# Inverse sums behind the third mask, four PSUM banks for the last batch's turns, and bounds of experts read ahead of the routed loop

## The reference, cut to what matters

```python
x = x + self_attention(layernorm(x), w_atten, w_proj)   # 16 heads of 32, rope on q and k, causal softmax
x = x + cross(layernorm(x), ctx)                        # energy = (ctx Wq + bq)(ctx Wk + bk)^T, softmax,
                                                        # then layernorm(x) @ attention: tokens are mixed
h = layernorm(x)
shared = silu(h @ Ws_gate) * (h @ Ws_up) @ Ws_down      # inner width 704, every token
scores = softmax(h @ W_router)                          # 8 experts, the best 2 of each token
routed = sum over the 2: score * ffn_e(h)               # inner width 352
x = x + routed + shared
```

## Time and profile before

| | us |
|---|---|
| median of 3 runs | 995.3 (993.45 to 995.39) |
| the profiled execution | 993.71, its span 991.9 |
| PE busy | 954.6 (96%) |
| DVE busy | 624.6 (63%) |
| ACT busy | 492.1 (50%) |
| POOL busy | 207.1 (21%) |

### The profile page before, as it was taken

One profiled execution on the slowest core, in us unless ns is written; L12 is line 12 of the kernel. 1 busy time (PEld: TensorE's weight loads), 2 busy tenths in 40 slices (PEclk: granted clock), 3 DMA queues, 4 the chain that ended last, 5 costly groups with the idle time before them and its releaser, 6 DMA issues.

```text
span 991.9 us, 18270 instructions
## 1 busy us (share of the span) xinstructions
PE 954.6 (96%) x6147; PEld 770.8 (78%) x6147; DVE 624.6 (63%) x1644; ACT 492.1 (50%) x1289; POOL 207.1 (21%) x247
## 2 busy tenths in 40 slices
PE   8989899999999999999799999999999999999998
PEld 6457666766667676666588888899999999999997
DVE  5699777867878667787665676524443344425565
ACT  1478865746657466567843331334443344432221
POOL 3222212221122211120000002222322222203342
PEclk9999999999999999999999999999999999999999
DMA  9765754338643375446900121745534542515554
GB/s 244 116 99 75 157 111 66 57 50 241 122 65 54 51 208 114 65 65 225 317 27 22 61 78 54 268 151 172 162 103 144 172 152 88 170 50 162 169 174 157
DMA packets 69981, 124.94 MB, mean 126 GB/s; under 512 B 6352, under 2 KB 22992, under 8 KB 69904
## 3 DMA queue, kind: packets, MB, share of 16 engines
q1 hardware_dynamic: 63440, 104.81, 42.5%
q0 software_dynamic: 5600, 18.35, 6.4%
q10 hardware_dynamic: 864, 0.79, 0.5%
HBM read 70.19 MB, written 28.57 MB: 100 GB/s over the span
## 4 chain that ended last, share of the span: by engine, by line
PE 80%; DVE 9%; DMA 4%; issue 3%; ACT 3%; POOL 1%; DVEq 0%; ACTq 0%; POOLq 0%
PE ps L1432 26%; PE ps L1442 14%; PE ps L1181 8%; PE ps L1341 5%; PE ps L1279 5%; PE ps L1233 5%; PE ps L1220 3%; DMA ks<-rope_a 3%; PE ps L1256 3%; PE ps L1206 3%; PE ps L1450 2%; PE ps L1420 2%; PE ps L1122 1%; DVE probs L1617 1%; DMA qs<-rope_b 1%
## 5 line engine op out<-in xcount | busy, mean ns | idle before, releaser
L1617 DVE CUSTOM_DVE_ANT_0 probs<-ps,mask 128x128 f32<-128x128 f32 (+3 forms) x256 | 122.3, 486 | 64.6 <-PE ps L1220 32.9
L910 ACT COPY probsT<-ps 128x128 f32<-128x128 f32 (+3 forms) x256 | 108.7, 425 | 103.5 <-PE ps L1233 64.2
L902 ACT ACTIVATE probs<-probs,nb 128x128 f32<-128x128 f32 (+3 forms) x256 | 146.6, 573 | 23.9 <-DVE nb L1622 23.4
L1220 PE MATMUL ps<-ks,qs 96*128 96x256 f32 (+2 forms) x256 | 127.1, 500 | 10.1 <-DVE mx L1617 7.5
L1233 PE MATMUL ps<-ident,probs 128*128 128x128 f32 x640 | 112.8, 275 | 1.6 <-ACT probsT L910 1.4
L1028 ACT ACTIVATE sg<-ps 128x352 f32<-128x352 f32 x69 | 32.0, 464 | 159.8 <-PE ps L1432 158.3
L1233 PEld LDWEIGHTS ps<-ident,probs 128*128 128x128 f32 x640 | 78.7, 141 | 26.9 <-issue 18.9
L1922 DVE TENSOR_TENSOR hidden<-sg,ps 128x352 f32<-128x352 f32 x69 | 35.8, 519 | 95.7 <-ACT sg L1028 95.7
L781 POOL TENSOR_TENSOR rope_a<-rope_a,sin_sb 128x512 f32<-128x512 f32 (+1 forms) x34 | 41.2, 1210 | 226.4 <-DVE rope_a L1599 226.4
L1220 PEld LDWEIGHTS ps<-ks,qs 96*128 96x128 f32 x256 | 48.5, 190 | 49.9 <-DVE mx L1617 21.2
L1926 DVE TENSOR_TENSOR h_lo<-ps,h_hi 128x384 fp32r<-128x384 f32 x68 | 37.9, 557 | 74.3 <-ACT h_hi L1032 73.6
(11 more groups left out here) (226 smaller groups left out, 2139.8 us busy)
## 6 DMA issues: line engine op xcount, KB each, us to landing
gu_raw<-in_we SPq DMA_DIRECT2D x10, 1408.0 KB, 6.6
y_d<-y_sb SPq DMA_DIRECT2D x37, 256.0 KB, 2.8
shared_x<-xT_d SPq DMA_DIRECT2D x32, 256.0 KB
qs<-rope_b SPq DMA_DIRECT2D x30, 256.0 KB, 5.7
ks<-rope_b SPq DMA_DIRECT2D x30, 256.0 KB, 5.7
d_raw<-in_we SPq DMA_DIRECT2D x10, 512.0 KB, 8.3
attT<-in_wpT SPq DMA_DIRECT2D x4, 1024.0 KB, 8.6
acc<-in_x SPq DMA_DIRECT2D x4, 1024.0 KB, 10.8
```

The source lines that it names most:

```text
L902: nc.scalar.activation(pr, pr, ACT.Exp, bias=nb[:, n % 2, h:h + 1], scale=SCALE, accum_out=sums[:, n % 2, h:h + 1]).then_inc(exp_done, 1)
L910: nc.scalar.copy(probsT[n % 2][:, h, 0:w], ps[:, T_BANK + h % 2, 0:w]).then_inc(pT_done, 1)
L1220: nc.tensor.matmul(ps[:, S_BANK + h % 2, 0:w], stacks[G % 2][0][:, h, i * P:(i + 1) * P], stacks[G % 2][1][:, h, 0:w], start=True, stop=Tr ...
L1617: nc.vector.tensor_tensor_reduce(probs[n % TT][:, h, 0:w], ps[:, S_BANK + h % 2, 0:w], mask[:, TOKENS - w:], 1.0, LOWEST, ALU.add, ALU.max ...
```

## The change

Five edits. First, `invert(n)` on DVE moves from ahead of the second mask (h = 1) to behind the third (h = 2) of the same step. Second, the last batch's turns of attention, second norm and third norm take four banks instead of two (`LAST_BANKS`: X_BANK, X_BANK + 1, T_BANK, O_BANK), so that tile t no longer waits for tile t - 2; the waits move to the reader before in the same bank: turns of the second norm wait for the attention copy of their own tile, turns of the third for the second norm's copy of their own tile, and `mix` waits for each tile's second copy. Third, LAST_CROSS changes places: attention turns, scales and second turns come up to a place sooner, the second energy a place later, the split of the projection's weights one or two places sooner. Fourth, PE, ACT and DVE read the end of expert 0 at FFN place 44, and of later experts one bound instead of two (the old end is the new beginning); SP still reads both. Fifth, on PE the second routed tile of expert 0 is written out ahead of the loop, and its gate, up and turn stand ahead of the wait for the last shared sum.

```diff
 LAST_CROSS = dict(
-    CROSS, context=(2, 7), context_copy=(7, 9), energy=(10, 11, 14, 15), energy_max=(10, 11, 14, 15),
+    CROSS, context=(2, 7), context_copy=(7, 9), energy=(10, 12, 14, 15), energy_max=(10, 12, 14, 15),
     energy_exp=(12, 14, 15, 16), energy_divide=(14, 18, 19, 20),
-    split_projection=(5, 6, 8, 10), split_y=(14, 14, 15, 16),
+    split_projection=(4, 5, 6, 8), split_y=(14, 14, 15, 16),
     project=((16, 16, 17, 18), (18, 18, 19, 19), (20, 20, 21, 21), (22, 22, 23, 23)), add_projected=(18, 20, 22, 24),
-    second_stats=(19, 21, 23, 25), second_variance=(26,), attention_turn=(25, 26, 27, 27), attention_copy=(25, 26, 27, 28),
-    second_scale=(28, 28, 29, 29), second_turn=(30, 30, 31, 31), second_copy=(30, 31, 31, 32),
+    second_stats=(19, 21, 23, 25), second_variance=(26,), attention_turn=(25, 25, 26, 26), attention_copy=(25, 26, 26, 27),
+    second_scale=(27, 28, 28, 29), second_turn=(29, 29, 30, 30), second_copy=(29, 30, 30, 31),
     mix=((33, 33, 34, 34), (35, 35, 36, 36), (37, 37, 38, 38), (39, 39, 40, 40)), add_mixed=(35, 37, 39, 41),
     third_stats=(36, 38, 40, 42), third_variance=(43,), third_scale=(45, 45, 46, 46), third_turn=(47, 47, 48, 48),
...
+        LAST_BANKS = (X_BANK, X_BANK + 1, T_BANK, O_BANK)
+
+        def turn_bank(p, t):
+
+            return LAST_BANKS[t] if p == BATCHES - 1 else X_BANK + t % 2
+
         def second_bank(p, t):
-            return X_BANK + (t % 2 if p == BATCHES - 1 else 1)
+            return LAST_BANKS[t] if p == BATCHES - 1 else X_BANK + 1
         SPLIT_PLACES = tuple((BATCHES - 1) * PLACES + at for at in (51, 52, 53, 55, 65, 67))
...
+        RANGE_PLACE = 44
+
+        def first_end(eng):
+
+            eng.wait_ge(slots_ready, 2)
+            return eng.value_load(first_i[0:1, 1:2], min_val=LEAST, max_val=ROUTED_TILES)
+
+        def next_end(eng, e):
+
+            return eng.value_load(first_i[0:1, e + 1:e + 2], min_val=LEAST, max_val=ROUTED_TILES)
+
         x_v = x.rearrange("(b t p) d -> b p t d", p=P, t=TT)
         out_v = out.rearrange("(t p) d -> p t d", p=P)
...
                         nc.scalar.copy(dst[:, :, t * P:(t + 1) * P],
-                                       ps[:, X_BANK + t % 2, :].rearrange("p (c n) -> p c n", c=TT)).then_inc(done, 1)
+                                       ps[:, turn_bank(p, t), :].rearrange("p (c n) -> p c n", c=TT)).then_inc(done, 1)
                     for t in tiles_at(since, 0, when["second_copy"]):
                         if p:
...
                     for t in tiles_at(since, 0, when["third_copy"]):
-                        copy_turned(norm3, p, t, xn_xT[:, t, :, :], X_BANK + t % 2, norm3.copied)
+                        copy_turned(norm3, p, t, xn_xT[:, t, :, :], turn_bank(p, t), norm3.copied)
                     if since in when["router_copy"]:
                         act.wait_ge(r_mm, p + 1)
...
                     hidden_high(shared, j - 1)
+                if place == RANGE_PLACE:
+                    hi = first_end(act)
                 if place in SILU_PLACES:
                     nc.scalar.activation(silu_unused[:], bias_sb[:, 0:1], ACT.Silu)
...
             hidden_high(shared, TILES - 1)
-            act.wait_ge(slots_ready, 2)
             for e in range(EXPERTS):
-                lo, hi = block_range(act, e)
-                if e == 0:
-                    lo = 0
+                lo, hi = (hi, next_end(act, e)) if e else (0, hi)
                 act.wait_ge(raw_loaded, (e + 3) * RAW)
                 split(e + 2, e % 2, range(SOONER))
...
                         pe.wait_ge(norm2.copied, p * TT + t)
-                elif t < 2:
-                    pe.wait_ge(aT_done, p * TT + t + 3)
                 else:
-                    pe.wait_ge(norm2.copied, p * TT + t - 1)
+                    pe.wait_ge(aT_done, p * TT + t + 1)
                 turn_tile(norm2, p, t, second_bank(p, t))
...
                     pe.wait_ge(xm_added, p * TT + t + 3)
+                elif p < BATCHES - 1:
+                    pe.wait_ge(norm3.copied, p * TT + t - 1)
                 else:
-                    pe.wait_ge(norm3.copied, p * TT + t - 1)
-                turn_tile(norm3, p, t, X_BANK + t % 2)
+                    pe.wait_ge(norm2.copied, p * TT + t + 1)
+                turn_tile(norm3, p, t, turn_bank(p, t))
             def project_qk(G, i, chunks, bank, cols=slice(0, TOKENS)):
...
                     pe.wait_ge(proj_added, p * TT + t + 3)
-                else:
+                elif p < BATCHES - 1:
                     pe.wait_ge(aT_done, p * TT + t - 1)
                 for c in range(TT):
-                    last = nc.tensor.transpose(ps[:, X_BANK + t % 2, c * P:(c + 1) * P],
+                    last = nc.tensor.transpose(ps[:, turn_bank(p, t), c * P:(c + 1) * P],
                                                xn[:, t, c * P:(c + 1) * P], ident[:])
                 last.then_inc(aT_mm, 1)
...
                 if 0 in chunks:
+                    if p == BATCHES - 1:
+                        pe.wait_ge(norm2.copied, p * TT + t + 1)
                     if t == 0:
                         pe.wait_ge(aT_done, p * TT + TT)
-                        pe.wait_ge(norm2.copied, p * TT + (1 if p < BATCHES - 1 else 3))
+                        pe.wait_ge(norm2.copied, p * TT + 1)
                         if p + 2 < BATCHES:
                             pe.wait_ge(xnT_low_done, (p + 1) * TT + 3)
                     elif t == 1:
-                        pe.wait_ge(norm2.copied, p * TT + TT)
+                        if p < BATCHES - 1:
+                            pe.wait_ge(norm2.copied, p * TT + TT)
                     else:
                         pe.wait_ge(xm_added, p * TT + t - 1)
...
                         last.then_inc(table_mm, 1)
+                if place == RANGE_PLACE:
+                    hi = first_end(pe)
                 j, step = shared_step(place)
                 if j >= 0 and step == 0:
...
                     turn_hidden(shared, j)
-            pe.wait_ge(slots_ready, 2)
             for e in range(EXPERTS):
                 pe.wait_ge(lo_made, (e + 2) * WC)
-                lo, hi = block_range(pe, e)
-                if e == 0:
-                    lo = 0
+                lo, hi = (hi, next_end(pe, e)) if e else (0, hi)
                 gate_up(routed, lo, (e + 1) % 2)
                 turn(routed, lo + 1)
...
                 if e == 0:
+                    gate_up(routed, 1, 1)
+                    turn(routed, 2)
                     pe.wait_ge(shared.y_out, TILES + 1)
-                with pe.Fori(lo + 1, hi) as j:
+                    down(routed, 0, 1)
+                    turn_hidden(routed, 1)
+                with pe.Fori(lo + 1 if e else LEAST, hi) as j:
                     gate_up(routed, j, (e + 1) % 2)
                     turn(routed, j + 1)
...
                             cols = slice(t * P, (t + 1) * P)
-                            nc.vector.tensor_tensor(att_low[:, :, cols], ps[:, X_BANK + t % 2, :].rearrange("p (c n) -> p c n", c=TT),
+                            nc.vector.tensor_tensor(att_low[:, :, cols], ps[:, turn_bank(p, t), :].rearrange("p (c n) -> p c n", c=TT),
                                                     att_high[:, :, cols].bitcast(F32), ALU.subtract).then_inc(aT_done, 1)
                     if since in when["second_variance"]:
...
                 r, h = divmod(place, GH)
-                n = step_at(place, INVERT_LAG)
-                if h == 1 and n is not None:
-                    invert(n)
                 if r < ALL_STEPS:
                     mask_and_max(r, h)
+                n = step_at(place, INVERT_LAG)
+                if h == 2 and n is not None:
+                    invert(n)
                 n = step_at(place, WEIGH_LAG)
                 if h == GH - 1 and n is not None and n % TT == TT - 1:
...
                         turn(routed, 0)
+                if place == RANGE_PLACE:
+                    hi = first_end(dve)
                 if j >= 1 and step == 0:
                     if j >= 2:
...
             for e in range(EXPERTS):
-                lo, hi = block_range(dve, e)
-                if e == 0:
-                    lo = 0
+                lo, hi = (hi, next_end(dve, e)) if e else (0, hi)
                 for i in range(SOONER):
                     low_part(e + 2, e % 2, i)
...
```

## The result

| | us |
|---|---|
| before, median of 4 runs | 994.97 (993.45 to 995.39) |
| the changed kernel, median of 4 runs | 987.77 (987.12 to 988.89) |
| ratio, 95% interval | 0.9922 (0.9903 to 0.9942) |
| forecast | 989.6, range 986.3 to 993.6 |

The account below looks back on a forecast made before the run. PE bounds the kernel (80% of the chain), so only its idle time can be won: inverse -2.8, last batch -0.25, bounds and peeled tile -1.85, together -4.9 us; from 994.5 this gives 989.6 us, range 986.3 to 993.6.

Parts of the forecast that it names:

- seven such, 5.5 us together: Attention: PE's gaps at scores behind the second mask, which stands behind the inverse's copy; 5.5 us winnable at most.
- the three fourth-mask waits: Attention after 113 us: the moved inverse delays fourth masks PE already waits for, three places by 0.39, +1.2 us.
- Rival 2: Attention: PE waits for the later inverse at 16 tight turns or behind fourth masks; slower, 998.6 us; chance 0.06.
- Rival 1: Attention: the inverse's gains are absorbed by stack transfers and fourth-mask waits; 992.6 us; chance 0.20.
- The rule on the shared ports: Copies beside POOL's roots, batches 1 to 3: held by GpSimd's exclusive lock, 1.0 us less gain; forecast held them free.
- (a): Last batch: the projection's weight splits now stand ahead of the router's work, delaying PE's next product, +0.8 us.
- (b): Last batch: the turn of `hidden` comes 1.2 us earlier, but three energy products now follow it, -0.4 us.
- (c): Last batch: four banks remove gaps of 1.05 and 1.02 at the third turns of attention and second norm, -2.1 us.
- (d): Last batch: the first two scaled tiles are turned sooner, so PE waits for the root's scales, +1.4 us.
- The gaps of 1.11 and 0.76: PE's idle time ahead of expert 0, by register loads and for the last shared sum; both expected to go.
- later experts lose one warm load each that was hidden: Experts after the first: one bound read fewer at each entry was expected to win PE nothing.
- rival 3: Bounds read at FFN place 44: the cold load stalls PE 1.3 us there; 990.9 us, rounded to 991; chance 0.10.

Follow-up runs that it names:

- the tenth run: The changed kernel with expert 0's second routed tile back in the loop, behind the wait for the last shared sum; ratio to before 0.9926.
- e1: The kernel before with only the inverse moved behind the third mask; ratio to before 0.9956, -4.4 us.
- e4: The changed kernel with its last-batch part undone (banks, waits and places as before); ratio to before 0.9938.
- e9: The kernel before, inverse at its old place, one reciprocal doing the 128x128 spread itself without the copy; ratio to before 1.0022.
- e3: The kernel before with only the bounds read ahead, one bound per later expert, and the peeled tile; ratio to before 0.9946.
- e7: The kernel before, inverse at its old place, the spread written as a two-operand maximum in place of the copy; ratio to before 1.0019.
- e11: The kernel before, inverse at its old place, the spread a reduction over a one-element axis in place of the copy; ratio 0.9952, -4.8 us.

## Why the prediction was right, and where its terms were off

**The inverse: right in sign and cause, mis-sized, -2.8 against -4.4 measured.** The failed step is "seven such, 5.5 us together": I read what a stall costs from PE's rows. The weight load of the same score waits too, and its row says more. Before, timeline of the weight loads, with the gap in brackets:

```profile
186.32 0.19 PEld L1220 LDWEIGHTS ps<-ks,qs 96*128 96x128 f32 x1 [1.05 <-DVE mx L1617]
...
244.94 0.19 PEld L1220 LDWEIGHTS ps<-ks,qs 96*128 96x128 f32 x1 [0.37 <-DVE mx L1617]
...
370.82 0.19 PEld L1220 LDWEIGHTS ps<-ks,qs 96*128 96x128 f32 x1 [0.38 <-DVE mx L1617]
```

At 186 PE's own row says 0.82, and the changed kernel won 1.01 there; at 244.94 and 370.82 PE's rows print no gap (the trace holds 0.13 and 0.14 us), and 0.40 and 0.42 were won. The ends of matmuls are modelled and hide 0.24 us of each of these waits, and more of two others: at 62.02, where PE's row says 0.92, the load's gap fell from 1.74 to 0.31, and the score came 1.43 sooner.

```profile
62.01 0.19 PEld L1220 LDWEIGHTS ps<-ks,qs 96*128 96x128 f32 x1 [1.74 <-DVE mx L1617]
```

```profile
59.96 0.19 PEld L1236 LDWEIGHTS ps<-ks,qs 96*128 96x128 f32 x1 [0.31 <-DVE mx L1639]
```

Nine gaps of the weight loads sum to 9.1 us where PE's seven rows had 5.5. The load's gap is not a price by itself either: at 154.79 and 402.59 it is 0.56 and 0.55 with none on PE; both went, the score came 0.3 sooner each time, and the next score had given it back.

To 113 us the forecast was -1.6 and the trace says -1.5; all of the shortfall lies behind it, -1.2 against -3.2 (of which some 0.4 is in the trace with before's own attention too). What I said of the rest held: the gap at 62.02 was absorbed by the stack's transfer (-2.06 at the score before, -0.53 at the group's first), the group after it kept 1.6 (-2.12), and the three fourth-mask waits grew by 0.35, 0.46 and 0.35 where I had 0.39, as at the earlier trace rows:

```profile
224.01 0.50 PE L1236 MATMUL ps<-ks,qs 96*128 96x512 f32 x1 [0.59 <-DVE mx L1639]
```

Rival 2 shows itself in two places only, 0.17 and 0.34 us at the turns of the inverse. Rival 1 fell. One more reading was off and cost nothing: 14 of the new copies are held, for 5.1 us in all, where 11 and 3.0 were laid out; the run with the reduction behind the third mask shows that this is off PE's way.

**The rule on the shared ports, weighed beside the root.** I held a copy there free, by the short bias of the earlier trace rows. The changed kernel has such a copy:

```profile
179.11 1.01 POOL L785 TENSOR_TENSOR norm_rstd<-norm_veps,power 128x4 f32<-128x4 f32 x1
...
179.35 0.23 DVE L1653 COPY inverse<-rsum 128x128 f32<-128x128 f32 x1
```

0.23 us, within the root; so too at 302.44 and 424.55. The rule, which in the Trainium skill (same page and section) has the lock held for a whole instruction, does not hold for this small operation, though it does for the rope's 128x512 ones.

**The last batch: -0.25 forecast, 0.0 measured (0.9999).** The times can't tell the two apart. By the traces (a) +0.8 was 0.9, (b) -0.4 was -0.39, and (c) and (d) -0.65 were -0.48 in the tenth run. What the sum had no term for: PE's idle time of 1.4 and 0.4 us in (d) can be followed by 3.4 us at half clock, worth 1.6. The profile of before had no fall while PE worked, and so no row warned of it.

**Bounds and the peeled tile: -1.87 forecast, some -3.7.** Two steps failed. The gaps of 1.11 and 0.76 of the earlier trace rows were read in PE's rows again; the weight loads have 1.34 and 1.00, and 1.38 and 1.07 were won.

```profile
633.81 0.30 PEld L1432 LDWEIGHTS ps<-gu_hi,routed_xT_hi 128*128 128x128 f32 x2 [1.34 <-issue]
```

And "later experts lose one warm load each that was hidden" is wrong: each entry had a gap on the weight loads that PE's row hides.

```profile
668.69 0.30 PEld L1432 LDWEIGHTS ps<-gu_hi,routed_xT_hi 128*128 128x128 f32 x2 [0.16 <-issue]
```

The seven entries, 0.14 to 0.19 each by the traces, are 1.1 of the 1.27 us. That the load at place 44 would be unseen was right (rival 3 fell): no gap follows it, and it took less than the 1107 ns I allowed.

```profile
L553 PEldq TENSOR_LOAD <-first_i x1: 492/492/492, 615.4 to 615.4; - x1
```

**The total** lies nearer than its terms, and that is luck in part. Two terms were short by the same misreading, 1.6 us (by the times) for the inverse and 1.8 for the bounds, 3.4 together, while the total is off by 1.8 (989.6 against 987.77). On the other side stand the last batch and the clock falls that the changed kernel's executions have too; how much of the median these are was not measured apart. Two small slips stand in the sum: the third part enters as -1.85 and not -1.87, and 994.5 less 7.5 is 987.0, not 986.8; neither changes the forecast.

## What to carry to other kernels

Read what a stall of TensorE costs from the weight load's row beside the matmul's: here the matmul's fell short by 0.24 us or more each time, and two waits of 0.37 and 0.38 by the load were not printed for the matmul at all. Where only the load waited (0.55 us, twice), nothing was to be won, so check against the next instructions' starts. Before moving a short VectorE instruction out of the way of GpSimd, look for a form of it that the trace shows unheld; one that reduces over an axis of one gave the same gain without any move. Where two kernels differ by under 2 us, compare the starts of the same instructions and the granted clock of each stretch before believing a median, and do it with a second execution of the old kernel too: here the same attention differed by 0.5 us between traces.

## What was not expected of the hardware

A small GpSimd operation (128x4, 1.01 us) doesn't hold a VectorE copy that a 128x512 one holds up to 1.1 us. A VectorE reciprocal of 128x128 takes 0.945 us, where a copy takes 0.227 and a reduction over one element 0.286. After PE had idled once for 1.0 to 2.0 us the granted clock in some traces fell to 0.50 for about 3.4 us, worth 0.7 to 1.6 us, and in others with the same idle time at the same instruction it did not: behind the 2.00 us ahead of the turn of `hidden` it fell in three traces (e1, e4, e9) and stayed in four (before, e3, e7, e11). Which it will be, no run here tells, and that stays open.
